# Pairing the steps of two attention loops: four score products, then two weighings, with the extra products dealt unevenly

## The reference

```python
scores = jnp.einsum('bqhd,bkhd->bhqk', Q, K) / math.sqrt(D_K)
scores = jnp.where(causal, scores, -jnp.inf)
attn = jax.nn.softmax(scores, axis=-1)
out = jnp.einsum('bhqk,bkhd->bqhd', attn, V)
...
kv_cum = jnp.cumsum(phi_k[..., :, None] * v[..., None, :], axis=2)
num = jnp.einsum('bhtf,bhtfd->bhtd', phi_q, kv_cum)
den = jnp.einsum('bhtf,bhtf->bht', phi_q, jnp.cumsum(phi_k, axis=2))[..., None] + EPS
```

## Time and profile before

| | |
|---|---|
| median of three runs | 2960.91 us |
| the profiled execution, and its span | 2961.86 us, 2959.7 us |
| mean granted TensorE clock | 0.938 of full speed |
| TensorE matmul busy | 2508.8 us, 85% |
| VectorE busy | 2276.6 us, 77% |
| ScalarE busy | 1784.9 us, 60% |
| softmax attention, about | 263 to 1216 us |
| second attention, about | 2084 to 2692 us |

### The profile page before, as it was taken

One profiled execution on the slowest core, in us unless ns is written; L12 is line 12 of the kernel. 1 busy time (PEld: TensorE's weight loads), 2 busy tenths in 40 slices (PEclk: granted clock), 3 DMA queues, 4 the chain that ended last, 5 costly groups with the idle time before them and its releaser, 6 DMA issues. The chain is left out here.

```text
span 2959.7 us, 60061 instructions
## 1 busy us (share of the span) xinstructions
PE 2508.8 (85%) x15239; PEld 1160.4 (39%) x15239; DVE 2276.6 (77%) x5893; ACT 1784.9 (60%) x2938; POOL 577.6 (20%) x650
## 2 busy tenths in 40 slices
PE   2687999999999999577999978884899999995656
PEld 1342333333333333254666655553222222222545
DVE  5887888888888888286777767997667666665968
ACT  0452666666666666315777747664677777773446
POOL 0445111111121111230000001222222222222300
PEclk9897999999999999888999999997899999997879
DMA  5495232332323322240000003445644444442403
GB/s 169 155 286 187 83 92 89 91 93 86 107 80 100 94 86 79 85 168 1 0 0 0 0 1 100 156 146 167 161 142 141 137 136 139 140 127 99 142 15 113
DMA packets 243316, 309.97 MB, mean 105 GB/s; under 512 B 39472, under 2 KB 177408, under 8 KB 243200
## 3 DMA queue, kind: packets, MB, share of 16 engines
q1 hardware_dynamic: 242752, 307.50, 33.6%
q10 hardware_dynamic: 448, 1.31, 0.2%
HBM read 181.29 MB, written 126.88 MB: 104 GB/s over the span
## 5 line engine op out<-in xcount | busy, mean ns | idle before, releaser
L893 ACT ACTIVATE a_p<-psum 128x1024 f32<-128x1024 f32 (+3 forms) x768 | 588.1, 813 | 303.0 <-PE psum L996 298.4
L893 ACT ACTIVATE b_p<-psum 128x512 f32<-128x512 f32 (+5 forms) x768 | 453.5, 654 | 164.4 <-PE psum L996 163.5
L948 DVE CUSTOM_DVE_ANT_0 a_dump<-psum,a_bias 128x128 bf16<-128x128 f32 (+3 forms) x1024 | 445.6, 487 | 105.7 <-PE psum L985 74.4
L996 PE MATMUL psum<-b_qs,b_ks 96*128 96x512 bf16 (+7 forms) x1536 | 320.9, 330 | 36.0 <-DMA b_vs<-values 35.7
L946 DVE TENSOR_REDUCE a_peak<-psum 128x1 f32<-128x512 f32 x512 | 326.1, 685 | 21.7 <-PE psum L985 20.2
L1010 PE MATMUL psum<-b_p,b_vs 128*32 128x512 f32 (+3 forms) x3072 | 328.5, 499 | 8.0 <-POOL b_p L866 8.0
L925 DVE COPY b_twin<-psum 128x512 f32<-128x512 f32 (+3 forms) x384 | 213.5, 556 | 146.6 <-PE psum L996 144.9
L985 PE MATMUL psum<-a_ks,a_qs 112*128 112x128 bf16 (+2 forms) x1008 | 294.0, 336 | 37.9 <-DVE a_peak L948 19.9
L866 POOL TENSOR_SCALAR_AFFINE_SELECT a_p<-a_p 128x512 f32<-128x512 f32 x256 | 162.4, 635 | 767.2 <-ACT a_p L893 767.2
L866 POOL TENSOR_SCALAR_AFFINE_SELECT b_p<-b_p 128x512 f32<-128x512 f32 x256 | 162.4, 634 | 455.2 <-DVE b_p L928 440.2
L996 PE MATMUL psum<-a_qs,a_ks 114*128 114x512 bf16 x1008 | 248.0, 328 | 3.4 <-ACT a_p L893 1.8
(11 more groups left out here) (202 smaller groups left out, 3752.8 us busy)
## 6 DMA issues: line engine op xcount, KB each, us to landing
qk_parts<-l_parts SPq DMA_DIRECT2D x96, 256.0 KB
qk_parts<-g_parts SPq DMA_DIRECT2D x96, 256.0 KB, 2.8
b_qs<-qk_parts SPq DMA_DIRECT2D x160, 128.0 KB, 2.9
b_ks<-qk_parts SPq DMA_DIRECT2D x155, 128.0 KB, 2.9
values<-l_vx SPq DMA_DIRECT2D x64, 256.0 KB
sums<-a_osb SPq DMA_DIRECT2D x64, 256.0 KB, 2.4
m_num<-sums SPq DMA_DIRECT2D x64, 256.0 KB
m_inv<-reciprocals SPq DMA_DIRECT2D x64, 256.0 KB
```

Source lines behind the costliest of these rows:

```text
L893: act.activation(p[s % SLOTS][:, 2 * k:2 * k + heads, q0(s):512], m.psum[:, at:at + heads, q0(s):512], ACT.Exp if softmax else ACT.Square, ...
L948: last = dve.tensor_tensor_reduce(dump[c % SRING][:, at:at + w], piece, bias[:, 512 - w:], 1.0, NEG, ALU.add, ALU.max, dst)
L996: last = pe.matmul(m.bank[score_bank(s, hd)][:, q0(s):512], ks[r][live, hd, kt * P:(kt + 1) * P], qs[r][live, hd, h * 512 + q0(s):(h + 1) ...
```

## The change

1. In both attentions the loop over steps goes in twos. TensorE now does the score products of steps s + 2 and s + 3 (four calls) and then the weighings of steps s and s + 1.
2. In the softmax attention the 36 chunks are dealt by a table: one or two after each of the four score calls, none between the weighings and none between a weighing and the next score call. `MOST` gives the numbers for each of the six pairs of steps: 5, 6, 8, 7, 5 and 5 chunks.
3. In the softmax attention the hardware loop has 15 units in its body and goes round twice, on every engine. In the second attention it stays at three units and ten rounds.

```diff
+    LAPS = 5 if softmax else 1
+    LONG = RING * LAPS
...
+    MOST = ((1, 1, 1, 2), (1, 2, 1, 2), (2, 2, 2, 2), (2, 1, 2, 2), (1, 1, 1, 2), (1, 1, 1, 2))
...
-            with eng.Fori(0, ROUNDS) as i:
-                for r in range(RING):
-                    unit(RING * i + r, r, i, True, True)
+            with eng.Fori(0, ROUNDS // LAPS) as i:
+                for j in range(LONG):
+                    unit(LONG * i + j, j % RING, LAPS * i + j // RING, True, True)
...
-                for s in range(STEPS):
-                    t = s + AHEAD
-                    there = t < STEPS or ahead
-                    if t == STEPS and ahead:
-                        operands(n + 1, (r + 1) % RING, rnd + (r + 1) // RING)
-                    at = (n, r, t) if t < STEPS else (n + 1, (r + 1) % RING, t - STEPS)
-                    if there:
-                        scores(*at, 0)
-                    some_maxima(3 * s)
-                    if there:
-                        scores(*at, 1)
-                    some_maxima(3 * s + 1)
+                dealt = 0
+                for s in range(0, STEPS, 2):
+                    for t in (s + AHEAD, s + AHEAD + 1):
+                        if t == STEPS and ahead:
+                            operands(n + 1, (r + 1) % RING, rnd + (r + 1) // RING)
+                        at = (n, r, t) if t < STEPS else (n + 1, (r + 1) % RING, t - STEPS)
+                        for k in range(2):
+                            if t < STEPS or ahead:
+                                scores(*at, k)
+                            if softmax:
+                                for _ in range(MOST[s // 2][2 * (t - s - AHEAD) + k]):
+                                    some_maxima(dealt)
+                                    dealt += 1
                     weigh(n, r, s)
-                    some_maxima(3 * s + 2)
+                    weigh(n, r, s + 1)
```

More of the change, by code:

```diff
@@ L711, in attend_pass @@
     HPU, ST, UNITS = z.HPU, z.ST, z.UNITS
+    LAPS = 5 if softmax else 1
+    LONG = RING * LAPS
+    assert (UNITS - 2) % LONG == 0
     ROUNDS = (UNITS - 2) // RING
-    assert UNITS == RING * ROUNDS + 2
     ROWS = STACK + 2 if softmax else STACK
@@ L730, in attend_pass @@
     CH = 2 * CP
-    assert CH == 3 * STEPS
     SRING = 3
     EARLY = 9
+    MOST = ((1, 1, 1, 2), (1, 2, 1, 2), (2, 2, 2, 2), (2, 1, 2, 2), (1, 1, 1, 2), (1, 1, 1, 2))
+    assert len(MOST) == STEPS // 2 and sum(map(sum, MOST)) == CH
     with ExitStack() as ctx:
@@ L1021, in some_maxima @@
                 def some_maxima(k):
-                    if not softmax:
-                        return
                     half = CH // 2
```

## The result

The changed kernel takes 3187.3 us (median of four runs, 3186.55 to 3189.83) against 2959.07 for the kernel before (four runs, 2954.92 to 2962.0). The ratio is 1.077, with a 95% interval of 1.0755 to 1.0793: slower by 228 us. Forecast were 3150 us and a range up to 3200. So the direction and the main mechanism came out, and 37 us were missing from the sum.

A forecast was written before the change was run, and what follows sets the result against it. It took TensorE as nearly always busy, with a load chain plus the work behind its wait setting each softmax unit. To 2961.9 us it added 122 (softmax attention) and 67 (second): 3151, so 3150 us, range 3060 to 3200.

The forecast's parts named there:

- the chain with its moved wait: Softmax attention: load chain of 15.67 us sets the unit; 2.13 us more work moves behind its wait; TensorE idles 3.4 us.
- the clock: Softmax attention: nine in ten load waits drop TensorE's clock, 1.62 us a fall, so 1.46 us a unit.
- The rival that the clock holds: Softmax attention: the 3.4 us idle costs no clock fall, 42 us less, 3108 us; chance 0.15.
- the waits of the score calls: Both attentions: score calls wait for ScalarE's bank, back after 1.78 us; 1.80 us a softmax unit, 3.98 in the second.
- the 21.03 forecast: Second attention: a unit goes from 18.94 to 21.03 us, +67 us over 32 units.
- weighings in a row: Both attentions: two weighings in a row cost nothing between them, so changes of kind halve, saving 1.58 us a unit.
- The last rival: Both attentions: weighings in a row keep their 0.147 us turnaround, +45 us, 3195 us; chance 0.05.
- VectorE's ring: Softmax attention: chunks wait a little for VectorE's three banks; 0.2 us a unit, bounds 0 and 0.6.
- I cost it at nothing: Softmax attention: the 15-unit loop body removes eight of nine VectorE stalls of 2.50 us, yet changes the time by nothing.
- no row shows any: Softmax attention's long loop body: more code in a row could cost instruction fetches, but no profile row shows such a cost.
- already absorbed: Softmax attention: VectorE's stalls at loop turns lie ahead of the load wait, so a three-unit round takes three load chains.
- the load in time: Softmax attention rival: SyncE's chain shortens below 12.25 us, a unit takes 28.16 us, total 3006 us; chance 0.07.

The follow-up runs named there:

- experiment 1: The changed kernel with the softmax attention's loop body back at three units: 3165.55 us, ratio 1.069 against the kernel before.
- Experiment 5: The changed kernel with loads issued ahead of the sums' store and, from the loop's fourth unit, only the values' transfer issued: 3053.89 us, ratio 1.033.
- Experiment 6: The kernel before with only the softmax attention's loop body lengthened to 15 units: 2996.72 us, ratio 1.0125.
- experiment 7: The kernel before with loads issued ahead of the sums' store and bodies of 15 units, SyncE's kept at three: 2918.39 us, ratio 0.986.
- experiment 10: The kernel before with the pair order in the second attention alone, ScalarE squaring only a quarter of each call's columns there: 2966.24 us, ratio 1.002.

## Why the prediction was right or wrong

The softmax parts side by side, in us, one execution each:

| kernel | softmax part |
|---|---|
| before | 902.4 |
| before, loop body of 15 | 931.8 |
| before, early loads | 881.8 |
| before, early loads, body of 15 except on SyncE | 854.5 |
| after | 1075.0 |
| after, body of 3 | 1047.2 |
| after, 19th chunk one place later | 971.1 |
| after, early loads | 999.5 |
| after, next to no load wait | 936.9 |

**Right: the chain with its moved wait.** The idle of 3.4 us is met, and moving the chunk back takes away 104 of the 172.6 us (1075.0 - 971.1). This one position in the order costs more than all listed waits for ScalarE (29.4 + 6.0 us here, 62.5 in the second attention).

**Right: the clock.** Nine falls in ten were forecast; 26 of 28 came. The rival that the clock holds is out. A wait near 3 us is no sure fall: waits of 2.6 and 3.0 us passed without one in the changed kernel, and three of 2.7 to 3.0 in experiment 1. Behind the wait the stretch takes 19.3 us in the mean against 17.6 in the two units that held: 1.7 a fall, for 1.62.

**Right: the waits of the score calls.** A bank came back after 1.72 us (second attention), for 1.78. Six waits a unit that are 0.06 us shorter make 0.36 of the 0.43 us by which a unit there stayed under the 21.03 forecast. Steps 0 and 1 of a unit went as worked out: 3.50 us from first call to weighings (705.39 to 708.89) for 3.56.

**Right: weighings in a row.** Two of width 512 take 2395.67 - 2393.81 = 1.86 us to the next call, which is 2 x 0.853 and one turnaround of 0.15, not two. This holds against the rule of the Trainium skill (TensorE: Matmul & The Clock Gate, Part 3, The mechanism) that a weight load overlaps only where its row group differs: all these weighings use all rows. The same section also lets a load go ahead into the background weight buffer; the row would fit that, and no run tells which it is. The last rival is out.

**Wrong in size: VectorE's ring, taken at 0.2 us a unit.** I said that the calls already wait for ScalarE. They do, but the chunks wait again at the ends of the pairs: steps 8 and 9 take 4.08 us from first call to weighings for 3.56, steps 10 and 11 take 2.64 for 2.29. That is some 0.85 for the 0.2, in the unit that I read, and above my bound of 0.6. Experiment 5 says the same: behind the awaited chunk a unit takes 16.72 us without a fall, where the terms of the prediction give 15.91. Part of it is a chunk that waits for ScalarE behind a call, which I had left out:

```profile
703.43 0.39 PE L988 MATMUL psum<-a_ks,a_qs 112*128 112x512 bf16 x1 [0.25 <-ACT a_p L896]
```

**Wrong: the long body, "I cost it at nothing", and "no row shows any".** It costs 22 to 33 us in the kernels with late loads, where SyncE has it too. A smaller part is the load chain. In the changed kernel it is 15.21 us from store to awaited chunk, leaving out the one turn of SyncE's loop, where it is 19.54. Before it was 14.71 in the 20 units that waited for the load. The issues make 0.4 of these 0.5: 10.06 to 10.48. The larger part is the clock, which falls more often behind the longer waits (experiments 1 and 6). I looked at VectorE alone, while SyncE is the engine on which this path lies. Why single issues take 0.9 to 1.9 us is not shown; they come with long bodies on the other engines even where SyncE's is short (experiment 7). That instructions are fetched late is only argued.

**Wrong: the round's stalls as "already absorbed".** That "a round of three units takes no longer than three load chains" does not hold for the kernel before. In nine of 28 units, those where the loop has gone round, TensorE reached the awaited chunk without a load wait. These took 17.32 us from last weighing to chunk, and the others 15.86. So 1.46 us of a stall showed, nine times: 13 us. The sum of 27.98 us for a measured 28.97 was short partly by this: 0.47 a unit for these nine, 0.28 for five falls, 0.19 because I read the chain from one unit. It did the forecast no harm: the 33.04 us were summed without a stall, and the changed kernel has one turn of the loop in place of nine. Experiment 6 shows what the long body comes to on the kernel before: these stalls go, and it is 33 us slower all the same.

**Together.** Measured less forecast is 34.70 - 33.04 = 1.66 us a unit, or 48 us over 29 intervals. In the prediction's own terms, as means of 28 units:

| term | forecast | measured |
|---|---|---|
| last weighing to awaited chunk | 15.67 | 16.20 |
| behind the chunk, without falls (experiment 5) | 15.91 | 16.72 |
| falls of the clock | 1.46 | 1.72 |

The 0.53 of the first line are 0.19 because I read the chain from one unit, 0.15 for the one loop end, and 0.4 for SyncE's issues, less 0.28 because the sums' copy starts sooner (0.11 us after the last weighing instead of 0.38). The 0.81 of the second are VectorE's ring and the chunks behind a call. That gives 1.60 of the 1.66. Against the 48 us the second attention was 12 us cheaper than the 67 forecast, which leaves 36 of the 37 us. That two errors had opposite signs was luck, and the time came to lie only 13 us under the top of the range. The shares are read from one execution, good to about 0.1 each.

**Wrong, unseen in the total: the load in time.** For this rival I gave a unit of 28.16 us. Experiment 5 has 29.50: 12.78 ahead of the chunk for 12.25, and 16.72 behind it for 15.91, since both have more waits for VectorE than I counted. What the load wait hides cannot be read off a sum of calls.

Open are why single issues take long, the last 7 us of experiment 10, and what a body of 15 on SyncE would cost with early loads.

## What to carry to other kernels

Grouping like matmuls saves the turnarounds, here 0.26 us each, only if the engines behind the buffers keep up with the burst. Here two or three bank pairs against four calls gave back more than was saved, three pairs against three calls did so too, and the next buffer in line (VectorE's) was nearly as tight. Before moving work, find the instruction that waits for the longest chain of transfers and keep ready work ahead of it: one chunk's place was worth 100 us. A longer loop body is to be priced on the path that bounds the unit: here it gained 22 us where TensorE waited for VectorE's stalls, and lost 22 to 33 where it waited for the load.

## What the runs showed of the hardware

- The granted clock of TensorE can fall to its lower level after waits of only 1.65 to 2 us, but not every time: behind 5 of 20 load waits before, 19 of 29 with the long body alone (waits of 2.1 us in the mean), 27 of 29 in the changed kernel (3.4 us). Waits of up to 3.0 us passed without a fall. A fall costs 1.6 to 1.7 us.
- Where a hardware loop goes round, VectorE stood still for 2.50 to 2.87 us before, and 3.2 to 3.5 with early loads. SyncE, with 15 units in its body, issued its first transfer 2.9 to 3.0 us late and took 1.6 us longer for the 15. At the turn of the long body TensorE waited 3.0 to 4.0 us for nothing that the profile shows ("issue").
- With 15 units in the bodies of the other engines, 11 to 22 of 435 transfers took 0.9 to 1.9 us to issue, whether SyncE's body had 3 units or 15; with 3 units on all engines 0 to 3 did, and most take 0.33 to 0.67.
